# A 32-bit projection operand in place of two 16-bit halves, in a chain of four convolution layers

## The reference

```python
# layer 0 (ternarize: each weight becomes -alpha, 0 or +alpha)
h = relu6(bn(conv(x, ternarize(w1))))                      # 1x1, 32 -> 192 channels
h = relu6(bn(conv(h, ternarize(w2), padding=1)))           # 3x3, 192 -> 192 channels
x = x + bn(conv(h, ternarize(w3)))                         # 1x1, 192 -> 32 channels: the projection
# layer 1: two 3x3 convolutions on 8-bit quantized input and weights, 32 -> 32; its first step is max(x)
# layers 2, 3: 3x3 convolution 32 -> 32, bn, relu, and channels with a small maximum set to zero
```

## Time and profile before

| what | value |
|---|---|
| time, median of 3 runs | 337.96 us (337.7 to 338.82) |
| profiled execution, its own time | 337.9 us |
| its span, first to last instruction | 336.1 us |
| mean granted TensorE clock | 0.974 |
| PE busy | 273.8 us, 2333 matmul records |
| DVE busy | 270.7 us, 494 instructions |
| ACT busy | 177.2 us |
| layer 0's slots | some 48 to 248 us of the span |

### The profile page before, as it was taken

One profiled execution on the slowest core, in us unless ns is written; L12 is line 12 of the kernel. 1 busy time (PEld: TensorE's weight loads), 2 busy tenths in 40 slices (PEclk: granted clock), 3 DMA queues, 4 the chain that ended last, 5 costly groups with the idle time before them and its releaser, 6 DMA issues.

```text
span 336.1 us, 5992 instructions
## 1 busy us (share of the span) xinstructions
PE 273.8 (81%) x2333; PEld 148.9 (44%) x2333; DVE 270.7 (81%) x494; ACT 177.2 (53%) x253; POOL 39.5 (12%) x43
## 2 busy tenths in 40 slices
PE   1131729999999999999999999799998997485863
PEld 1110305555554555554555554455545554253422
DVE  4599999799797988877988877786357587999983
ACT  2643226748546547555546664758215565526651
POOL 1698490000000000000000000003000000000111
PEclk9999978999999999999999999999999999979779
DMA  7333321000000000000000000000000000222132
GB/s 212 147 79 80 78 59 43 2 3 0 0 2 3 0 2 0 2 1 0 0 0 0 0 0 2 0 3 0 2 0 2 0 0 2 56 57 58 51 105 96
DMA packets 5575, 9.62 MB, mean 29 GB/s; under 512 B 1712, under 2 KB 3952, under 8 KB 5552
## 3 DMA queue, kind: packets, MB, share of 16 engines
q1 hardware_dynamic: 5280, 8.82, 9.7%
q10 hardware_dynamic: 272, 0.49, 0.6%
HBM read 3.60 MB, written 1.61 MB: 15 GB/s over the span
## 4 chain that ended last, share of the span: by engine, by line
PE 61%; DVE 22%; ACT 6%; issue 5%; DMA 3%; POOL 1%; ACTq 0%; DVEq 0%
PE ps L436 13%; PE ps L432 9%; PE ps L422 9%; PE ps L461 7%; PE ps L457 5%; PE ps L446 5%; PE ps L569 4%; PE ps L399 3%; DVE va L950 3%; PE ps L600 2%; DVE big L1205 2%; DMA par<-params_in 2%; PE ps L476 2%; ACT big L803 2%; DVE hp L942 1%
## 5 line engine op out<-in xcount | busy, mean ns | idle before, releaser
L436 PE MATMUL ps<-hb,w2bt 128*128 128x392 f16 x288 | 55.6, 337 | 0.0
L432 PE MATMUL ps<-vh,w2at 128*128 128x392 f16 x192 | 38.8, 339 | 6.4 <-DVE ps L980 6.4
L600 PE MATMUL ps<-big,wst 128*32 128x392 f16 x576 | 30.1, 371 | 16.4 <-ACT vh L817 10.8
L399 PE MATMUL ps<-xk,w1t 96*128 96x392 bf16 (+1 forms) x64 | 22.2, 357 | 19.8 <-ACT part L648 14.4
L422 PE MATMUL ps<-vh,wu 128*128 128x392 f16 x192 | 37.1, 345 | 1.4 <-DVE vh L956 1.4
L436 PEld LDWEIGHTS ps<-hb,w2bt 128*128 128x128 f16 x288 | 28.0, 97 | 22.5 <-issue 1.1
L950 DVE TENSOR_TENSOR va<-hp 128x420 f32<-128x420 f32 x64 | 37.6, 649 | 0.4
L666 ACT CAST vh<-va 128x1680 f16<-128x1680 f32 x16 | 25.3, 1582 | 17.5 <-DVE va L950 17.5
L648 ACT ACTIVATE ra<-ps,bn 128x392 f32<-128x392 f32 x32 | 21.4, 678 | 24.1 <-PE ps L399 24.0
L648 ACT ACTIVATE part<-ps,bn 128x392 f32<-128x392 f32 x32 | 21.7, 679 | 22.6 <-PE ps L399 22.4
L956 DVE TENSOR_TENSOR vh<-va,vh 128x1680 f16<-128x1680 f32 x16 | 30.5, 1908 | 0.5
(11 more groups left out here) (200 smaller groups left out, 450.2 us busy)
## 6 DMA issues: line engine op xcount, KB each, us to landing
xk<-xpart SPq DMA_DIRECT2D x45, 49.0 KB, 1.9
big<-big SPq DMA_DIRECT2D x4, 450.0 KB, 3.9
xin<-x_in SPq DMA_DIRECT2D x4, 392.0 KB, 8.1
y_out<-xin SPq DMA_DIRECT2D x3, 392.0 KB, 2.4
big<-w2a_in SPq DMA_DIRECT2D x3, 288.0 KB, 7.0
big<-w2b_in ACTq DMA_DIRECT2D x1, 432.0 KB, 6.8
y_out<-xin SPq DMA_DIRECT2D x2, 196.0 KB, 2.0
wqr<-wq_in SPq DMA_DIRECT2D x8, 36.0 KB, 1.9
```

The lines of the kernel that those rows point to most:

```text
L399: nc.tensor.matmul(ps[:, bank, :HALF], (w1t[:, 0:P], w1t[:, P:P + 2 * HB])[two], xk[:, j, HALF * h:HALF * h + HALF], start=True, stop=True ...
L432: nc.tensor.matmul(ps[:, PBANK[k], :HALF], weights(k, dx, False), vh[:, b, part, k, :, dx:dx + W], start=False, stop=False, skip_group_che ...
L436: i = nc.tensor.matmul(ps[:, PBANK[k], :HALF], w2bt[:, t, 0:P], rows(b, k // 3, t), start=False, stop=(t == TAPS - 1), skip_group_check=True)
L600: i = nc.tensor.matmul(ps[C * g:C * g + C, bank + h, :HALF], wst[:, layer, C * t:C * t + C], kst[:, layer, c % 2, g, r0:r0 + HALF_ROWS, dx ...
```

## The change

The clamped second activation stays in 32 bits: h2a and h2b lose their hi/lo dimension and become F32, of the same size in bytes. The two subtractions on DVE and the semaphore between clamp and subtraction are gone. w3t becomes F32. `project` has two steps in place of four, each with four 32-bit matmuls, and both waits stand ahead of the steps. After the last slot the h2a steps of both calls are followed by the h2b steps of both.

```diff
-        w3t = sb("w3t", [P, 2, C], F16)
+        w3t = sb("w3t", [P, 2, C], F32)
...
-        h2a = sb("h2a", [P, G, 2, HW], F16)
-        h2b = sb("h2b", [P, G, 2, HALF], F16)
+        h2a = sb("h2a", [P, G, HW], F32)
+        h2b = sb("h2b", [P, G, HALF], F32)
...
-        h1 = h2a[:].rearrange("p g k f -> p g (k f)").bitcast(F32)
+        h1 = h2a
...
-            def project(c, h, steps=(0, 1, 2, 3), bank=7):
+            def project(c, h, steps=(0, 1), bank=7):
 
                 wait(pe, y0_ready, 2 * c + h if bank == 7 else 0)
                 lower = slice(HB * h, HB * h + HB)
+                pe.wait_ge(h2a_ready, (c + 1) * G)
+                if 1 in steps:
+                    pe.wait_ge(h2_ready, (c + 1) * G)
                 for s in steps:
-                    if s < 2:
-                        pe.wait_ge((h2a_ready, h2_ready)[s], (c + 1) * G)
                     for g in range(G):
-                        w, rhs = ((w3t[:, 0, :], h2a[:, g, s, HALF * h:HALF * h + HALF]) if s < 2 else
-                                  (w3t[lower, 1, :], h2b[lower, g, s - 2, :]))
-                        i = nc.tensor.matmul(ps[C * g:C * g + C, bank, :HALF], w, rhs, start=(s == 0), stop=(s == 3))
-                if 3 in steps:
+                        w, rhs = ((w3t[:, 0, :], h2a[:, g, HALF * h:HALF * h + HALF]) if s == 0 else
+                                  (w3t[lower, 1, :], h2b[lower, g, :]))
+                        i = nc.tensor.matmul(ps[C * g:C * g + C, bank, :HALF], w, rhs, start=(s == 0), stop=(s == 1))
+                if 1 in steps:
                     i.then_inc(proj_done, 1)
...
             project(NCH - 1, 0, (0,))
             project(NCH - 1, 1, (0,), bank=6)
-            project(NCH - 1, 0, (1, 2, 3))
-            project(NCH - 1, 1, (1, 2, 3), bank=6)
+            project(NCH - 1, 0, (1,))
+            project(NCH - 1, 1, (1,), bank=6)
...
                 dve.wait_ge(r2a_ready, j + 1)
-                ts(h2a[:, g, 0, :], r2a[:], CAP, None, ALU.min).then_inc(h2hi_done, 1)
-                dve.wait_ge(h2hi_done, 2 * j + 1)
-                stt(h2a[:, g, 1, :], r2a[:], CAP, h2a[:, g, 0, :], ALU.min, ALU.subtract).then_inc(h2a_ready, 1)
+                ts(h2a[:, g, :], r2a[:], CAP, None, ALU.min).then_inc(h2a_ready, 1)
 
             def halves2_b(j, g):
                 dve.wait_ge(r2b_ready, j + 1)
-                ts(h2b[:, g, 0, :], r2b[:], CAP, None, ALU.min).then_inc(h2hi_done, 1)
-                dve.wait_ge(h2hi_done, 2 * j + 2)
-                stt(h2b[:, g, 1, :], r2b[:], CAP, h2b[:, g, 0, :], ALU.min, ALU.subtract).then_inc(h2_ready, 1)
+                ts(h2b[:, g, :], r2b[:], CAP, None, ALU.min).then_inc(h2_ready, 1)
```

More of the change, by code:

```diff
@@ L186, in conv_seq @@
             sem, ("hp_done", "v_ready", "va_ready", "hbhi_done", "hb_ready", "seed_a", "seed_b"))
-        h2hi_done, h2a_ready, h2_ready, y0_ready = map(
-            sem, ("h2hi_done", "h2a_ready", "h2_ready", "y0_ready"))
+        h2a_ready, h2_ready, y0_ready = map(sem, ("h2a_ready", "h2_ready", "y0_ready"))
         gm_go, gm_done, q_v, q_ready, q1_done, h1_ready, q2_done, t1_ready, ys_ready = map(
```

## The result

The changed kernel takes 345.47 us in the median of 4 runs (344.72 to 346.46), against 338.31 us in 4 runs of the kernel before: a ratio of 1.0216, with a 95% interval from 1.0188 to 1.0245. It is slower by 7.2 us, about 2%. Slower was forecast, but by 20; the profiled execution takes 344.72 us, with a span of 342.9 us against 336.1. Of the predicted cost on PE (16.0 us in the loop and 4.47 after it) about a quarter is there.

A forecast was written before the change was run, and what follows sets the result against it. PE was taken to bound the loop, so DVE's relief was worth nothing. Added projection time of +16.0 us in the loop and +4.0 net after it, on 337.9, gave 357.9 us; 342 to 362 held the first three cases, 0.82.

The forecast's parts named there:

- 16.0 us in the loop and 4.47 after it: Added PE time of the projection: six calls at +2.67 us each, then +4.47 for the last pair, net +4.0.
- Two records a matmul: In the projection, each 32-bit matmul appears as two records on the same column tile, so a call keeps 16 records.
- Half the rate per column: In the projection, 4-byte operands pass at about half the f16 rate: 0.336 us a record against 0.172.
- T: Time of one 32-bit record of 392 columns in the projection, taken as 0.336 us.
- The waits moved to the head of a call: Waits for h2a and h2b ahead of each projection call: no new PE wait in the loop, no cost.
- The cost of a change of shape: On PE, each switch between 128-wide and 64-wide work adds 0.10 us; two switches a call in the loop.
- 5T a step: In a projection step, lo waits for hi's column tile and holds up the next image's hi; a call takes 3.56 us.
- the last pair: The two interleaved projection calls after the loop: 6.25 us in 32 bits against 1.78, so +4.47.
- packed, two-pass: Rival for the projection: hi records of four tiles overlap, then lo ones; 1.54 us a call, +4.6, 342.5 us; chance 0.13.
- the staircase: Main case for the projection: records start one behind another, with two passes; 357.9 us, own range 355 to 361, chance 0.55.
- one pass a record: Rival for the projection: same staggered starts, 0.172 us a record; 1.92 us a call, 345.1 us; 0.08 of its 0.14.
- The residuals: After the loop: calls further apart leave DVE free for the second residual, so 0.46 us of the added time hides.

The follow-up runs named there:

- e3: The f16 kernel before, with every projection step of the six calls in the loop issued twice, eight rounds in place of four: 342.85 us, ratio 1.0133.

## Why the prediction was wrong

**Right.** What bounds the kernel: PE in the loop, and not DVE; two runs confirm it from both sides. Two records a matmul. Half the rate per column: T was put at 0.336 us and measured 0.354, twice the 0.177 of the same gap in f16, which is 0.05 to 0.07 us a call. The waits moved to the head of a call cost nothing. The cost of a change of shape, 0.10 us, held: a call without one is shorter by 0.11. The net effect is a loss.

**Wrong, and the cause of the miss:** the step "it waits, and the next image's hi is queued behind it", that is 5T a step. The run with f16 pairs shows that a matmul that waits for its tile doesn't hold up those for other column tiles, and the changed kernel's rows show the same in 32 bits; a step is 2T. That took 6 x 2.0 us from the sum in the loop, and 10 x 0.336 = 3.4 of the 3.95 us by which the last pair was put too high (6.25 against 2.30). The other 0.6 is the two h2b steps side by side, 2 x 0.336 = 0.7, less 0.1 for the larger T. I had called this "what issue in order and the four-fold overlap give together"; the overlap was in rows 4, the issue in order was in no row. The rival "packed, two-pass", at 342.5, had the mechanism of a call right and was given 0.13. The measured time lies in the range of 342 to 362, but not for the reason forecast: the staircase by itself had 355 to 361. The rival "one pass a record", at 345.1, comes within 0.4 us of the measured time by coincidence: it has a staircase and T = 0.172, and the traces show neither.

**From that rival to the measured time.** It lacks three things: T, 0.3 us in six calls; the stretch after the loop, 1.21 us more where it had 0.65, since it let 0.46 us hide and the second residual in fact came 0.69 later, while it put the calls at 2.89 us and they took 2.30; and the clock, 0.24 before the first call and 1.18 in the last stage. 342.5 + 0.3 + 0.56 + 1.42 is 344.8, and the profiled execution took 344.72.

**The residuals** were my second wrong step. I wrote that the calls would be further apart, and DVE free. The h2b steps of the two calls read different rows, 0 to 63 and 64 to 127, and write different banks, and the trace has their 16 records in flight together, in 0.89 us, so they finish together.

**What stays open.** The cause behind the 1.18 us of the last stage. That it is the clock, the rows show; why the clock fell for longer, they don't. In the eleven profiled executions the stage has 83.6 to 84.8 us, except for 86.2 in one; the five long ones (84.67 and more) have a low-clock stretch of 6.8 us in the last convolutions, and the next to last of these takes 5.67 to 5.78 us on the chain; the six short ones have a stretch of 3.4 us, and 4.58 to 4.92. The f16 kernel with padded weights on VectorE has 84.67 us there, without any 32-bit matmul, and the same kernel with them on GpSimd 83.94. So 32-bit operands aren't needed for it, and a later start alone (e3) doesn't bring it. Why all four profiled kernels with 32-bit matmuls have the long stretch, and of the seven in f16 only one, wasn't settled.

## What to carry to other kernels

A 32-bit matmul of this size costs four rounds of f16 time where a split into hi and lo costs two. It can pay only where the engine that makes the split is the one waited for, and the chain says that, not the busy share (81% on both engines here); no run here has such a case in the loop, so that side is reasoned and not shown. Matmuls on different column tiles, and on different row tiles with different banks, overlapped here even when the order of issue puts two on one tile back to back, so count the work of each tile and not the order. Look at what filling matmuls cover: here a third of them was enough, and that gave 1.4 us.

## What was unexpected

Four column tiles ran side by side with two consecutive records on each, at a cost of 3 ns a start (6.6 against 3.4 ns) and 0.02 us a call. Sixteen records on eight tiles (4 columns by 2 rows) took 0.89 us, where eight on four tiles take 0.87. And the spread between executions of one kernel, up to 4.8 us in twelve runs of the kernel with padded weights at mean clocks from 0.950 to 0.973, is larger than any of the smaller effects studied here; the kernel before spreads by 2.3 us in 23 runs.
